# Head rows of attention spread by SBUF-to-SBUF DMAs instead of selection matmuls and masked copies

## What is computed

```
def _mha(q_in, k_in, v_in, qw, qb, kw, kb, vw, vb, ow, ob, mask):
    q = (q_in @ qw + qb).reshape(b, sq, NHEAD, hd).transpose(0, 2, 1, 3)   # NHEAD 16, hd 8
    k, v = ...                                                             # likewise
    scores = einsum('bhqd,bhkd->bhqk', q, k) / sqrt(hd)
    if mask is not None: scores = where(mask == 0, -1e9, scores)
    out = einsum('bhqk,bhkd->bhqd', softmax(scores), v)
    return out.transpose(0, 2, 1, 3).reshape(b, sq, d) @ ow + ob
x = layernorm(x + _mha(x, x, x, ..., tgt_mask))
x = layernorm(x + _mha(x, ctx, ctx, ..., None))
x = layernorm(x + relu(x @ w1 + b1) @ w2 + b2)
Q_phi, K_phi = elu(x), elu(ctx)
attn = (Q_phi @ (K_phi^T ctx)) / (Q_phi . sum(K_phi) + 1e-6)
out = layernorm(x + attn)
```

## Time and profile before

| | |
|---|---|
| time, median of 3 runs (lowest to highest) | 346.71 us (345.96 to 347.55) |
| span of the profiled execution, first to last instruction | 345.9 us |
| PE busy, share of span | 297.7 us, 86% |
| DVE busy | 260.5 us, 75% |
| ACT busy | 175.4 us, 51% |
| POOL busy | 76.1 us, 22% |
| DMA queues of SP (q1) and ACT (q10), share of 16 engines | 6.2% and 0.2% |
| mean granted TensorE clock (1 is 2.4 GHz) | 0.952 |

### The profile page before, as it was taken

The page is one execution under the profiler, slowest core; times in us unless marked ns, Lnnn a source line. Parts: engine busy times, 40 slices in busy tenths (PEclk is TensorE's granted clock), DMA queues, the critical chain, the costliest instruction groups (busy, mean ns, idle before and its releaser), DMA issues.

```text
span 345.9 us, 8970 instructions
## 1 busy us (share of the span) xinstructions
PE 297.7 (86%) x3033; PEld 191.6 (55%) x3056; DVE 260.5 (75%) x867; ACT 175.4 (51%) x386; POOL 76.1 (22%) x136
## 2 busy tenths in 40 slices
PE   3778789989999999989998999899999997688551
PEld 2633555655665566656665666556656645454341
DVE  7563777877698889888897889888988884775424
ACT  2225445655565565646664666465664563336210
POOL 0500200211122112312231213112321223203321
PEclk9989999999999999999999999999999998689665
DMA  7500000000000000100000000000000000000000
GB/s 221 183 2 1 17 9 3 26 3 9 2 17 12 12 0 17 28 9 0 15 24 9 0 15 24 1 8 0 24 1 11 2 25 2 0 15 11 17 0 15
DMA packets 7506, 6.85 MB, mean 20 GB/s; under 512 B 744, under 2 KB 6712, under 8 KB 7480
## 3 DMA queue, kind: packets, MB, share of 16 engines
q1 hardware_dynamic: 7048, 6.38, 6.2%
q10 hardware_dynamic: 432, 0.14, 0.2%
HBM read 5.46 MB, written 1.05 MB: 19 GB/s over the span
## 4 chain that ended last, share of the span: by engine, by line
PE 68%; DVE 15%; issue 8%; ACT 3%; POOL 2%; DMA 1%; DVEq 1%; POOLq 0%; SPq 0%; ACTq 0%
PE av_ps L393 10%; PE proj_ps L422 10%; PE s_ps L377 6%; PE s_ps L359 5%; PE s_ps L381 5%; PE proj_ps L488 5%; PE proj_ps L447 4%; PE proj_ps L490 4%; PE s_ps L356 4%; PE proj_ps L428 3%; PE s_ps L375 3%; DVE neg_max L736 2%; PE post_ps L403 2%; POOL rstd L964 2%; PE post_ps L412 2%
## 5 line engine op out<-in xcount | busy, mean ns | idle before, releaser
L586 ACT ACTIVATE probs<-s_ps 128x512 f32<-128x512 f32 (+1 forms) x128 | 76.3, 596 | 51.8 <-PE s_ps L381 32.8
L736 DVE TENSOR_REDUCE neg_max<-s_ps 128x4 f32<-128x512 f32 (+1 forms) x128 | 71.6, 576 | 12.8 <-PE s_ps L359 12.4
L964 POOL TENSOR_TENSOR rstd<-var_e,neg_half 128x1 f32<-128x1 f32 x32 | 17.5, 548 | 183.8 <-DVE var_e L785 183.8
L381 PE MATMUL s_ps<-max_x,unit_sel 128*77 128x512 bf16 (+1 forms) x105 | 39.9, 380 | 0.0
L393 PE MATMUL av_ps<-probs,v_aug_s 128*32 128x128 f32 x512 | 27.3, 285 | 2.4 <-ACT probs L586 0.3
L356 PE MATMUL s_ps<-bias_q,id_b 128*128 128x512 bf16 x64 | 25.5, 398 | 4.2 <-DVE max_x L750 4.0
L422 PE MATMUL proj_ps<-x_t,w_sb 128*128 128x256 f32 x80 | 26.8, 458 | 0.6 <-issue 0.6
L393 PE MATMUL av_ps<-probs,v_aug_c 77*32 77x128 f32 x512 | 27.3, 285 | 0.0
L359 PEld LDWEIGHTS s_ps<-sk_rows,sq_wide 128*128 128x128 bf16 x256 | 20.5, 101 | 10.2 <-issue 1.7
L359 PE MATMUL s_ps<-sk_rows,sq_wide 128*128 128x128 bf16 x256 | 25.7, 225 | 0.0
L592 ACT COPY av_sb<-av_ps 128x256 f32<-128x256 f32 x32 | 11.9, 372 | 26.5 <-PE av_ps L393 26.5
(11 more groups left out here) (131 smaller groups left out, 663.3 us busy)
## 6 DMA issues: line engine op xcount, KB each, us to landing
xt_in<-in_x_t SPq DMA_DIRECT2D x8, 128.0 KB, 2.0
out<-o_all SPq DMA_DIRECT2D x8, 128.0 KB, 1.8
row_sb<-in_rows SPq DMA_DIRECT2D x1, 832.0 KB, 6.4
w_sb<-in_weights SPq DMA_DIRECT2D x1, 768.0 KB, 10.2
ct_in<-in_ctx_t SPq DMA_DIRECT2D x8, 77.0 KB, 1.8
cn_in<-in_ctx_n SPq DMA_DIRECT2D x8, 77.0 KB
w_sb<-in_weights SPq DMA_DIRECT2D x2, 128.0 KB, 3.0
id_f<-in_ident ACTq DMA_DIRECT2D x1, 64.0 KB, 2.5
```

Of the source, the lines that this page charges most:

```text
L381: nc.tensor.matmul(bank[0:n, :], unit_sel[:, u, 0:n], max_x[:, b, :, :], start=False, stop=True).then_inc(M["s2_ready"], 1)
L586: nc.scalar.activation(probs[0:n, u % 2, :], s2_ps[u % 2][0:n, :], ACT.Exp, scale=SCALE).then_inc(M["exp_done"], 1)
L736: nc.vector.tensor_reduce(neg_max[:, b, RH * u:RH * (u + 1)], scores, AX_X, ALU.max, negate=True).then_inc(M["max_done"], 1)
L964: nc.gpsimd.tensor_tensor(rstd[:, b, :], var_e[:, b, :], neg_half[:, 0:1], ALU.pow).then_inc(M["rstd_ready"], 1)
```

## The change

The selection matmuls, the copies and the masked copies go. `spread_part` lays the same rows out with DMAs from SBUF to SBUF. For each of the four combinations s there is one DMA that writes k's 32 rows with step 4 (64 KB for self-attention), and one for each head j that writes 8 rows of q (16 KB): 20 DMAs for a group and kind, 40 in a turn. The weights' columns are put into another order on the host, so that a head's channels lie where the DMA reads them. The rest of `wide` has to be zero and is set so once by two memsets on POOL (4096 float32 elements for each partition). `rows_k` and `wide` hold two groups, so that one can be filled while the other is read. Both sequences of a group lie in one tile.

SP issues the 20 DMAs of `sqk` behind the load of `ct_in`, and those of `cqk` as the last thing of a turn, each behind a wait for the low parts. In turn -1 ACT's queue issues half of them. PE waits for the DMAs' semaphore before the first query-major unit of a job (`wait_spread`). The eight spread entries leave `PROJ_USES`. All turns are written out; the hardware loop is gone.

```
-        ("yc0", TAIL, 0, 0), ("cv", CROSS, 0, 0), ("cq0", CROSS, 0, 1), ("ck0", CROSS, 0, 2), ("sqk", NEXT, 0, 3),
...
+        ("yc0", TAIL, 0, 0), ("cv", CROSS, 0, 0), ("sqk", NEXT, 0, 3),
...
+        for i in range(NEXT, NG + LAST):
             iteration(i)
...
+            rows_k[kind] = sb(f"{kind}k_rows", [P, 2, UNITS, G, KLEN[kind]], BF16)
+            wide[kind] = sb(f"{kind}q_wide", [P, 2, RH, UNITS, G, S], BF16)
...
+        SPREAD_DMAS = 4 + 4 * RH
+        def wait_spread(eng, kind, g):
+            eng.wait_ge(M[f"spread_{kind}"], 16 * SPREAD_DMAS * (g + 1))
+        def spread_part(eng, kind, g, s):
+            eng.dma_start(rows_k[kind][s:P:4, g % 2, :, :, :].rearrange("p u b n -> p u (b n)"),
+                          part_of(kind + "k", s)[:].rearrange("p b n -> p (b n)")).then_inc(M["spread_" + kind], 16)
+            for j in range(RH):
+                eng.dma_start(wide[kind][32 * j + s:32 * j + 32:4, g % 2, j, :, :, :].rearrange("p u b n -> p u (b n)"),
+                              part_of(kind + "q", s)[32 * j:32 * j + 32, :, :].rearrange("p b n -> p (b n)")).then_inc(
+                    M["spread_" + kind], 16)
...
+            def spread_rows(i, name):                      # on SP
+                kind = name[0]
+                g = i - (NEXT if kind == "s" else SELF)
+                wait_read(sp, i, name)
+                if g > 1:
+                    freed = job_index(g - 2, 2) if kind == "s" else job_index(g - 1, 4)
+                    sp.wait_ge(M["s2_ready"], UNITS * freed)
+                for s in range(2 if i == NEXT else 4):
+                    spread_part(sp, kind, g, s)
...
+                if on(i, NEXT):
+                    spread_rows(i, "sqk")
                 if on(i, LAST):
...
+                if on(i, SELF):
+                    spread_rows(i, "cqk")
...
                 if u == 0:
-                    pe.wait_ge(M[f"wide_{kind}"], G * g + b + 1)
-                    wait_rows(pe, kind, "k", b, g)
+                    wait_spread(pe, kind, g)
...
+                        if i == NEXT:                      # on ACT, behind split_hi
+                            act.wait_ge(M["wide_zero"], 2)
+                            wait_read(act, i, name)
+                            for s in (2, 3):
+                                spread_part(act, "s", 0, s)
...
+            for kind in "sc":                              # on POOL
+                nc.gpsimd.memset(wide[kind][:].rearrange("p h j u b n -> p (h j u b n)").bitcast(F32), 0.0).then_inc(
+                    M["wide_zero"], 1)
```

More of the change, by code:

```diff
@@ L110, in decoder_layer_kernel @@
     PROJ_USES = [
-        ("yc0", TAIL, 0, 0), ("cv", CROSS, 0, 0), ("cq0", CROSS, 0, 1), ("ck0", CROSS, 0, 2), ("sqk", NEXT, 0, 3),
[L112 to L116, removed]
+        ("yc0", TAIL, 0, 0), ("cv", CROSS, 0, 0), ("sqk", NEXT, 0, 3),
+        ("yc1", TAIL, 1, 0), ("h01", TAIL, 1, 1), ("h23", TAIL, 1, 2), ("ff", TAIL, 1, 4),
+        ("ys0", SELF, 2, 0), ("kv", TAIL, 2, 2), ("sv", NEXT, 2, 3), ("yt", TAIL, 2, 4),
+        ("ys1", SELF, 3, 0), ("cqk", SELF, 3, 2), ("la", TAIL, 3, 3)]
     USE_NAMES = [name for name, *_ in PROJ_USES]
@@ L142, in wait_reuse, with run_iterations @@
             eng.wait_ge(sem, value)
[L144 to L150, removed]
+    def run_iterations(iteration):
+        for i in range(NEXT, NG + LAST):
             iteration(i)
@@ L358, in query_major @@
                 for j in range(RH):
-                    last = nc.tensor.matmul(bank[:, j * n:(j + 1) * n], wide[kind][:, b, j, u, :],
-                                            rows_qk[kind + "k"][:, b, u, :], start=(kind == "c"), stop=True,
+                    last = nc.tensor.matmul(bank[:, j * n:(j + 1) * n], wide[kind][:, g % 2, j, u, b, :],
+                                            rows_k[kind][:, g % 2, u, b, :], start=(kind == "c"), stop=True,
                                             skip_group_check=True)
@@ L478, in linear_attention @@
                 last.then_inc(full("la"), 1)
-            def spread_rows(i, name):
-                kind, side, b = name[0], name[1], int(name[2])
-                n = KLEN[kind] if side == "k" else S
-                wait_read(pe, i if kind == "s" else i - 1, kind + "qk")
-                bank = open_bank(i, name)
-                for u in range(UNITS):
-                    nc.tensor.matmul(bank[:, u * n:(u + 1) * n], spread[side, "hi"][:, u, :, :],
-                                     hi[kind + side][:, b, :], start=True, stop=False)
-                    last = nc.tensor.matmul(bank[:, u * n:(u + 1) * n], spread[side, "lo"][:, u, :, :],
-                                            lo[kind + side][:, b, :], start=False, stop=True)
-                last.then_inc(full(name), 1)
             def light_work(i, k, u):
@@ L613, in split_hi @@
                 wait_full(act, i, name)
+                g = i - (NEXT if kind == "s" else SELF)
+                if g > 0:
+                    wait_spread(act, kind, g - 1)
                 for side, at, c in (("q", 0, C_SQB if kind == "s" else C_CQB),
@@ L805, in split_lo @@
                 last.then_inc(read(name), 1)
-            def widen(i, name):
-                key, b = name[:2], int(name[2])
-                wait_read(dve, i, name)
-                for j in range(RH):
-                    last = nc.vector.tensor_scalar(wide[name[0]][:, b, j, :, :], rows_qk[key][:, b, :, :],
-                                                   row_is_j[:, j:j + 1], None, ALU.mult)
-                last.then_inc(M["wide_" + name[0]], 1)
             def store_v(i, name, kind, bias):
@@ L848, in light_work @@
                 g = i - TAIL
-                for name in uses_at(i, k, u - 1):
-                    if is_spread(name) and name[1] == "q":
-                        widen(i, name)
                 for name in uses_at(i, k, u):
```

60 lines of the change are left out of this document (16 added, 44 removed).

## The result

| | before | after |
|---|---|---|
| median (lowest to highest) | 347.13 us (345.96 to 348.28), 4 runs | 423.71 us (421.93 to 424.25), 4 runs |
| ratio, 95% interval | 1 | 1.218 (1.211 to 1.225) |
| span of the profiled execution | 345.9 us | 422.1 us |
| PE busy, share of span | 297.7 us, 86% | 292.5 us, 69% |
| mean granted clock | 0.952 | 0.855 |

What follows compares the result with a forecast made beforehand. PE's own work was taken as the bound (busy 34.73 of 36.40 us a turn). Terms -2.3 + 1.9 + 2.6 + 0.9 + 1.0 + 2.0 + 2.7 = +8.8 on the 345.9 span: 354.7, median 355 us, range 334 to 372.

Steps and rivals of the forecast that it cites:

- an issue on SP: SP's time to issue each added DMA, taken as 0.46 us, so 9.2 us for 20.
- The upper bound, 0.88: SP's dearest comparable issue, the three-dimensional load x_all with its gap: 0.88 us, so 17.6 for 20.
- My own sign of being wrong: On SP's queue: the prediction is wrong if issues stand under 0.40 or over 0.52 us apart.
- Stretch C: PE's queue from projection cqk to projection sqk: 11.82 us before, 13.9 forecast, with PE waiting 2.8 for xt_in.
- Stretch S: PE's queue from projection sqk to the next self-attention's first query-major unit: 19.00 us before, 17.36 forecast, DMAs hidden.
- Full turns: Turns 2 to 6: 36.2 us each against 36.64 before, -2.3 us together.
- Turns 0, 1, 7, 8 and the prologue: Stretches with less work to hide DMAs: +1.9, +2.6, +0.9 and +1.0 us for the turns, +2 for the prologue.
- Clock: PE at half clock behind long waits, 1.35 us lost each; two losses charged, +2.7 us.
- B: Rival: SP's issues dearer, 0.55 us each, ten stretches grow 1.8 each plus clock losses; 380 us, chance 0.15.
- A: Rival: SP's issues cheap, change faster; at 0.37 us each 336 us, floor 324; chance 0.28, another 0.07 about break-even.
- C: Rival: POOL's two memsets in the prologue take 18 us, first unit at 25 instead of 14.9; 365 us, chance 0.10.
- unrolling counts nothing: Writing out the hardware loop's turns was forecast to change nothing, its end not being visible in PE's rows.

Runs made afterwards that it cites:

- experiment 2: Kernel before, with eight shapes of SBUF-to-SBUF DMA, four of each, issued by SP behind the last store; late rows 0.58 to 0.60 us, 8x4x256 0.67 to 0.69.
- experiment 6: Changed kernel with q's rows by four 32-partition DMAs and the masked copies kept on DVE, 8 DMAs a spread instead of 20; 341.61 us, ratio 0.984 to before.
- experiment 1: Kernel before with all turns written out instead of the hardware loop, nothing else changed; 345.53 us, ratio 0.997.
- experiment 9: Changed kernel with half of the DMAs of each spread issued on ACT's queue in every turn, the other ten on SP; 478.29 us, ratio 1.377 to before.
- experiments 4: Changed kernel with the 16 q-row DMAs left out of each spread, 4 issues instead of 20, scores wrong; 332.48 us, ratio 0.961 to before.
- 7: Kernel of experiment 6 with the load of xt_in ahead of the DMAs of cqk; 341.54 us, ratio 0.985 to before.

## Why the prediction was wrong

**The term that failed: an issue on SP.** "I take 0.46, next to the row that follows another directly: 9.2 us for 20." It is 0.64 and 0.715, in sum 14.0 us (experiment 2 and SP's rows). The row next to it was a load from HBM; what set these DMAs apart from it, that both ends are in SBUF and the elements two bytes wide, I did not weigh, and weighed dimensions and bytes, which do not count. The upper bound, 0.88, held the value. My own sign of being wrong, issues over 0.52 apart, is there. Of the rule of the Trainium skill quoted there, that initiating a DMA is usually small relative to the DMA itself, I said too much: one issue of 0.64 to 0.72 us is a third of the 2 us to landing. It is the row of twenty, 14.0 us, that is seven times as long, and the sentence of the page is about one DMA.

**Stretch C.** Forecast 13.9 us, measured 19.40. My own formula with the measured value: low parts at 2.58, twenty issues and the gap to `xt_in`'s 14.34, landing 2.48, sum 19.40. The structure was right to the last wait; the size was not.

**Stretch S.** Forecast hidden under 17.36 us of work, with the cover gone over 0.64 for an issue. Measured 19.56: no wait for a DMA shows in it, but it is longer by the low clock (3.42 us at half rate, 1.7 lost) and by `att`'s 0.71. Yet the cover is gone: with issues of 14.0 us my formula gives 2.88 + 13.3 + 2.0 + 0.1 = 18.3 (an estimate), more than the 17.36 of work, so without those 2.4 us PE would have waited for `sqk`'s DMAs, as it does where there is less work (47.89, with 7.41 us of waiting).

**Full turns.** Forecast 36.2 us, measured 44.32 in the one shown. From the `cqk` starts, turns 2 to 6 together gave +37.6 us instead of -2.3.

**Turns 0, 1, 7, 8 and the prologue.** Of the span's +76.2 us, 9.1 lie before the first `cqk` (forecast 3.9 and a part of the clock), 15.8 in turn 1 (2.6), 8.1 in turn 7 (0.9) and 5.6 behind it (1.0). Signs and places were right.

**Clock.** I charged two losses, though my own text named three waits longer than the 3.27 us of the earlier trace rows; there are eleven waits, and PE's rows behind each have the longer durations. The five losses in full turns, which I had left out of the sum, came, at some 1.7 each (half of 3.42). So the trace now agrees with the rule of the Trainium skill quoted in the prediction (TensorE: Matmul & The Clock Gate, HAM oscillation).

**Rivals.** B (dearer issues) was the case that came, beyond its assumed 0.55. By its rule, 14.0 - 9.2 = 4.8 us in ten stretches and five more losses of clock: 355 + 48 + 7 = 410. Of the other 14 us, 8 lie in turns 2 to 6 (219.6 us against 5 x 42.35 by that rule). I read them as S, which no longer gets shorter, and the stronger loss of clock; no run parts the two. I gave B 0.15 and a range up to 372; a range taken to the 0.88 that a row showed would have reached past 420, as the bounds of my own working demanded. A is refuted, since issues are not cheap, but its rule for C, that PE waits from 6.4 us of issues on, is borne out: in full turns there is no wait with 4 and 8 DMAs, and one of 1.75 to 2.6 us with 12 (some 8.3 us of issues). C did not come: the memsets took 7.0 us, near the 7.3 that I had reckoned, but not harmlessly (rows of POOL, then of DVE):

```profile
0.77 3.51 POOL L897 MEMSET sq_wide<- 128x4096 f32 x1
4.21 3.51 POOL L897 MEMSET cq_wide<- 128x4096 f32 x1
```

```profile
3.31 4.49 DVE L673 CAST id_b<-id_f 128x128 bf16<-128x128 f32 x1
```

A cast of 0.23 us stands until the second memset is over, at 7.8, and the first low part comes 1.7 us later than in experiment 6. That unrolling counts nothing was right (experiment 1).

## What to carry to other kernels

Count the issues, not the bytes: a row of n small DMAs on one queue takes n times the issue time (20 took 14.0 us here), and everything behind it in that queue, loads that used to be early above all, is late by the whole row. Whether the row is hidden is decided by the shortest stretch beside it, and beyond that point the cost bends upwards. Where no row shows a price, let the range reach to its upper bound, since it multiplies by every issue and every stretch. Replace matmuls by DMAs where a few do (eight of 32 partitions here gave 1.6%, and 2.6% with the large loads behind them, which is not clear of each other), leave to a compute engine with room what would need many, and do not let an engine that others wait for closely issue such a row (experiment 9). When a shared resource holds an instruction, moving the holder only helps where nothing urgent of the held engine follows.

## What the runs showed of the hardware

- An SBUF-to-SBUF DMA of bf16 takes SP 0.58 to 0.60 us to issue when others are ahead of it, whatever its size or dimensions, and with 8 partitions 0.67 to 0.69 (8x1024: 0.62 to 0.71), plus a gap of 0.04; on ACT's queue the rows of `cqk` took 0.60 to 0.71, and 0.68 to 0.77 with 8 partitions. A load of float32 from HBM in a full turn took 0.32 to 0.45, a store 0.40.
- A POOL instruction can hold a DVE instruction until it ends: DVE's masked copy and casts lasted 4.06 to 4.58 us beside a POOL instruction of 4.50 (or beside memsets of 3.51), while DVE's reductions out of PSUM kept their 0.68. The Trainium skill, page SBUF — State Buffer, section Who interferes with whom, says this: the two share a port pair as an exclusive lock, which copies, casts and `tensor_scalar` of DVE can take and `tensor_reduce` does not. The rows agree, and the kernel before has it too (masked copies of 2.60 instead of 1.14 us for four, ahead of its wait of 3.27).
- An SBUF-to-SBUF DMA issued while the last 768 KB of weights were under way took 4.3 to 6.0 us to land instead of 1.9, those on ACT's queue too, though the weights went by SP's (experiments 4, 6 and 7); with that load behind it, at most 2.9.
- POOL's memset of 4096 float32 for each partition takes 3.51 us, 0.86 ns an element.
